# First cross-attention: a new order of the jobs in a batch, and a table that gives each job its PSUM bank

## The chip, the cores and the metric

The kernel runs on one core of a Trainium2 chip: TensorE (PE), VectorE (DVE), ScalarE (ACT), GpSimd (POOL) and SyncE (SP), each with a queue of its own that it works through in order. The metric is device time in microseconds of one execution, as the median of several runs.

## What is computed

Two decoder layers of attention, cross-attention and feed-forward, each followed by a layer norm. Only the first cross-attention is touched. Cut to what matters:

```python
q = _ln((x @ Wq + bq).reshape(b, s1, H, HD), qn_w, qn_b)          # 16 heads of 32
kv = concatenate([y_main @ Wk + bk, y_main @ Wv + bv])             # 240 context rows
k = _ln(kv[..., :HD], kn_w, kn_b);  v = kv[..., HD:]
k_dca, v_dca = ...                                                # the same from the last 16 rows, own weights
ctx = softmax(q k^T * SCALE) v + softmax(q k_dca^T * SCALE) v_dca
x = _layernorm(x + ctx @ Wo + bo)
```

There are 8 batches of 256 rows, width 512. Both softmaxes run over the same 256 columns of scores: 240 and 16.

## The kernel before

`cross_attention_0` first prepares weights, then runs the 8 batches as a software pipeline. The work of a batch is cut into named jobs. A list (`order`) of jobs, each with a shift that says for how many batches ahead or behind it works, is one slot; `grouped_slots` makes 8 slots of it, and leaves out what would lie outside batches 0 to 7. `Plan` numbers the events. Every engine walks the same list and does its own part of each job, so the list sets the order on all five engines at once. The engines meet only through semaphores, whose counts `Plan` works out from the list.

The jobs, with u = 0 to 7 for four heads and one half of the rows, t or kt for a half of rows or keys:

- xt, yt: x or context is transposed on TensorE into a PSUM bank; ScalarE copies it, rounded, as the high half (L133), VectorE writes the rest as the low half (L139). All large products are three passes over such halves (L519).
- q(t), k(t), v(t): projections, 13 or 7 matmuls of 512 columns. For q and k ScalarE writes the squares and a copy (L919, L920), and VectorE makes the variance (L948, L950).
- qn, kn: GpSimd raises the variance to the power -0.5 and multiplies (L804, L806).
- qt, kt: four transposes; ScalarE writes a high half and a full copy (L895, L900). ql, kl: GpSimd subtracts them (L811).
- score(u): 12 matmuls into four banks kept for scores, of which there is one set, so score(u + 1) waits until exp(u) is over (L862). max(u): VectorE, the negated maximum (L954 to L960). exp(u): ScalarE, four exponentials with sums and one for the last 16 columns (L925, L928). rec(u): VectorE, the reciprocal sums (L965, L967). scale(u): GpSimd multiplies by them (L817).
- pt(u, kt): four transposes of the scaled result (L869), then high half and low half as above; av(m), m = 0 to 3: 24 matmuls of 256 columns; its result again as two halves.
- out(t): 13 matmuls; VectorE adds to x and takes statistics (L973, L163, L165), GpSimd takes the root, fin(t) applies it (L180).
- load: SyncE fetches the context of a later batch.

Four PSUM banks form a ring for all jobs but score. A job's matmuls wait until the bank's last user is read out: after the low half on VectorE, or for qt and kt after ScalarE. Which bank a job has comes from `turn`, which before is made by `bank_turns`: the ring jobs of a slot in their order take banks 0, 1, 2, 3, 0, ..., and the last three 0, 1, 2. Two temporary tiles (`temps`) are shared by q, k, qt, kt. Two tiles hold the exponentials, used by u in turn.

Of the kernel before, what the change touches and what calls it, by code (L numbers as in the profile page):

```python
# [522 lines left out]
def cross_attention_0(nc, g, ctx, a):  # L523
# [10 lines left out]
    def unit(u):
        return [(("score", u), 0), (("max", u), 0), (("exp", u), 0)]

    def turned(u, shift=0):
        return [(("pt", u, kt), shift) for kt in range(QT)]

    def ready(u):  # L540
        return [(("rec", u), 0), (("scale", u), 0)]

    order = [
        [(("ql", 0), 0), (("qt", 1), 0), *turned(7, -1), *unit(0), (("q", 0), 1), (("ql", 1), 0), *ready(0)],
        [*unit(1), (("qn", 0), 1), (("av", 3), -1), *ready(1), *turned(0), (("kt", 1), 0), (("v", 0), 0), (("kl", 1), 0)],
        [*unit(2), (("v", 1), 0), *ready(2), *turned(1), (("out", 0), -1)],
        [*unit(3), (("out", 1), -1), (("fin", 0), -1), (("av", 0), 0), *ready(3), *turned(2), (("yt",), 1), (("load",), 2)],
        [*unit(4), (("k", 0), 1), (("fin", 1), -1), *ready(4), *turned(3), (("k", 1), 1)],
        [*unit(5), (("kn", 0), 1), (("av", 1), 0), *ready(5), *turned(4)],
        [*unit(6), (("kn", 1), 1), (("q", 1), 1), *ready(6), *turned(5)],  # L550
        [(("score", 7), 0), (("kt", 0), 1), (("max", 7), 0), (("exp", 7), 0), (("qn", 1), 1), (("av", 2), 0), (("kl", 0), 1),
         *ready(7), *turned(6), (("xt", 0), 2), (("xt", 1), 2), (("qt", 0), 1)]]
# [1884 lines left out]
```

## Time and profile before

| what | value |
|---|---|
| median of 3 runs | 2538.05 us (2537.85 to 2539.27) |
| the profiled execution | 2538.91 us |
| its span, first to last instruction | 2537.0 us |
| mean granted TensorE clock | 0.933 |
| TensorE, VectorE, ScalarE, GpSimd busy | 2159.8, 1568.4, 1215.2, 762.9 us |
| the batches of the first cross-attention | about 505 to 1012 us of the span |

Starts are counted from the span's first instruction. A matmul's end in the trace is modelled and overlaps the next one's start, so spacing of starts, not the sum of durations, tells how long a run of matmuls took. An idle time is put down to the semaphore that came last.

### The profile page before, as it was taken

The page shows a single profiled execution, that of the slowest core. Times are in us where ns is not written, and L with a number is a line of the kernel's source. Part 1 is how long each engine was busy: PE and PEld are TensorE (multiplying, and loading weights), DVE is VectorE, ACT ScalarE, POOL GpSimd, SP SyncE. Part 2 cuts the span into 40 slices and gives each one's busy share as a digit, 9 for nine tenths or more (in the row PEclk, how much of TensorE's full clock was granted, in tenths as well). Part 3 has the DMA queues.
Part 4 walks back from the last instruction along what each step waited for, and adds up shares of the span by engine and source line. Part 5 has one row for each costly group of instructions (what it writes and reads, how often), then busy time and mean ns, then how long its engine had stood idle before and what let it go on. Part 6 is the DMA issues. An engine that isn't in the chain of part 4 may idle for free. (4 is left out here: it accounts for less than half of the span.)

```text
span 2537.0 us, 40781 instructions
## 1 busy us (share of the span) xinstructions
PE 2159.8 (85%) x15664; PEld 1831.0 (72%) x15664; DVE 1568.4 (62%) x3131; ACT 1215.2 (48%) x3223; POOL 762.9 (30%) x820
## 2 busy tenths in 40 slices
PE   5999998388888887499997879999999999966876
PEld 5898897266777766377776778888988988853443
DVE  3555664555656554788875645556666666656777
ACT  3555553366666653444333334445555554423466
POOL 2233332666666652044441111111111112220011
PEclk8999999689999987599998989999999999988999
DMA  3000000200000000711101031224324312101000
GB/s 133 1 2 1 2 1 1 75 5 5 5 5 6 5 1 4 256 65 34 34 18 46 1 133 59 93 84 145 113 84 146 112 68 76 51 1 67 6 29 34
DMA packets 42777, 127.17 MB, mean 50 GB/s; under 512 B 3917, under 2 KB 11086, under 8 KB 37593
## 3 DMA queue, kind: packets, MB, share of 16 engines
q1 hardware_dynamic: 42584, 124.56, 14.0%
q8 instruction: 126, 2.06, 0.4%
q14 instruction: 67, 0.54, 0.1%
HBM read 103.57 MB, written 20.97 MB: 49 GB/s over the span
## 5 line engine op out<-in xcount | busy, mean ns | idle before, releaser
L2003 POOL TENSOR_TENSOR x_probs<-x_probs,x_total 128x512 f32<-128x512 f32 x128 | 133.2, 1041 | 595.5 <-DVE x_total L1973 595.3
L1928 ACT ACTIVATE x_probs<-banks,x_nmax 128x256 f32<-128x256 f32 x256 | 119.0, 469 | 213.9 <-DVE x_nmax L1962 213.9
L133 ACT ACTIVATE x_probsT_hi<-banks 128x512 fp32r<-128x512 f32 x256 | 143.7, 607 | 106.8 <-PE banks L1862 101.2
L519 PE MATMUL banks<-x_probsT_hi,x_V_hi 128*128 128x256 f32 x512 | 160.6, 314 | 38.6 <-DVE x_probsT_lo L139 38.0
L139 DVE TENSOR_TENSOR x_probsT_lo<-banks,x_probsT_hi 128x512 fp32r<-128x512 f32 x256 | 165.1, 675 | 45.8 <-ACT x_probsT_hi L133 45.6
L519 PE MATMUL banks<-x_turned,x_wq_hi 128*128 128x256 f32 x1024 | 186.0, 283 | 8.2 <-DVE x_turned L139 8.2
L925 ACT ACTIVATE x_probs<-banks,x_nmax 128x240 f32<-128x240 f32 x256 | 114.4, 460 | 139.8 <-DVE x_nmax L955 139.8
L817 POOL TENSOR_TENSOR x_probs<-x_probs,x_total 128x960 f32<-128x960 f32 (+1 forms) x128 | 130.4, 1040 | 161.3 <-DVE x_total L967 161.3
L448 ACT ACTIVATE a_probs<-banks,a_nmax 128x128 f32<-128x128 f32 (+1 forms) x256 | 104.1, 419 | 126.9 <-DVE a_nmax L464 126.9
L519 PEld LDWEIGHTS banks<-x_turned,x_wq_hi 128*128 128x128 f32 x1024 | 156.8, 189 | 9.4 <-DVE x_turned L139 9.4
L504 POOL TENSOR_TENSOR a_probs<-a_probs,a_total 128x512 f32<-128x512 f32 x64 | 93.9, 1467 | 229.5 <-DVE a_total L474 229.5
L519 PE MATMUL banks<-x_probsT_lo,x_V_hi 128*128 128x256 f32 x512 | 154.7, 302 | 0.0
L519 PE MATMUL banks<-x_probsT_hi,x_V_lo 128*128 128x256 f32 x512 | 154.5, 302 | 0.0
L519 PEld LDWEIGHTS banks<-x_probsT_hi,x_V_hi 128*128 128x128 f32 x512 | 107.4, 210 | 51.0 <-DVE x_probsT_lo L139 49.7
L519 PE MATMUL banks<-x_turned,x_wq_lo 128*128 128x256 f32 x512 | 143.6, 280 | 0.0
L1279 POOL TENSOR_TENSOR f_hid_lo<-f_hid,f_hid_hi 128x256 fp32r<-128x256 f32 x128 | 93.8, 734 | 138.6 <-ACT f_hid_hi L133 138.6
L1260 ACT ACTIVATE f_act<-f_z 128x256 f32<-128x256 f32 x128 | 53.4, 417 | 149.8 <-DVE f_z L1331 149.8
L1242 PE MATMUL banks<-f_downT,f_hid_hi 128*128 128x512 f32 x256 | 111.0, 434 | 0.0
L519 PEld LDWEIGHTS banks<-x_probsT_hi,x_V_lo 128*128 128x128 f32 x512 | 108.2, 211 | 0.0
L519 PEld LDWEIGHTS banks<-x_probsT_lo,x_V_hi 128*128 128x128 f32 x512 | 107.9, 211 | 0.3
L519 PE MATMUL banks<-x_wo_hi,x_oT_hi 128*128 128x512 f32 x256 | 105.0, 410 | 2.1 <-DVE x_oT_lo L139 2.1
L140 DVE SCALAR_TENSOR_TENSOR x_qT_lo<-banks,x_qT_hi 128x512 fp32r<-128x512 f32 x64 | 44.3, 692 | 99.4 <-ACT x_qT_hi L133 99.4
(455 smaller groups left out, 7245.6 us busy)
## 6 DMA issues: line engine op xcount, KB each, us to landing
x_turned<-x_parked SPq DMA_DIRECT2D x24, 1536.0 KB, 6.8
x_parked<-x_turned SPq DMA_DIRECT2D x8, 1536.0 KB, 5.8
x_raw_q<-in_L_xattn_Wq_dram SPq DMA_DIRECT2D x5, 1024.0 KB, 5.2
x_raw_o<-in_L_xattn_Wo_dram SPq DMA_DIRECT2D x5, 1024.0 KB, 8.2
x_all<-in_x_dram SPq DMA_DIRECT2D x2, 2048.0 KB, 18.7
x_ys<-in_ctx_dram SPq DMA_DIRECT2D x16, 256.0 KB, 2.9
f_raw<-in_L_ffn_W_g_dram SPq DMA_DIRECT2D x4, 1024.0 KB, 7.0
f_raw<-in_L_ffn_W_u_dram SPq DMA_DIRECT2D x4, 1024.0 KB, 5.4
```

Source lines behind the costliest of these rows:

```text
L133: return eng.activation(out, in_, ACT.Copy, scale=scale)
L139: return eng.tensor_tensor(out, in_, high.bitcast(F32), ALU.subtract)
L448: ins = eng.activation(probs[u % NP][:, r, 0:keys], banks[:, r, :], ACT.Exp, bias=nmax[:, u, r:r + 1], accum_out=total[:, u, r:r + 1])
L504: eng.tensor_tensor(probs[u % NP][:, :, 0:keys], probs[u % NP][:, :, 0:keys], total[:, u, :].unsqueeze(2).to_broadcast([P, G4, keys]), ALU ...
L519: ins = eng.matmul(out, lhs, rhs, start=start and n == 0, stop=stop and n == len(steps) - 1)
L817: ins = eng.tensor_tensor(tile, tile, total[:, u, n, :].unsqueeze(2).to_broadcast([P, G4, c1 - c0]), ALU.mult)
L925: eng.activation(probs[u % NP][:, r, 0:MAIN], g.S[:, r, 0:MAIN], ACT.Exp, bias=nmax[:, u, r:r + 1], accum_out=total[:, u, 0, r:r + 1])
L1242: ins = eng.matmul(g.S[:, 2 * b.parity + t, :], h[:, t * P:(t + 1) * P], downT[:, m, :], start=m == 0 and n == 0, stop=m == HT - 1 and n == 1)
L1260: eng.activation(act[zb][:, :], z[zb][:, :], ACT.Silu).then_inc(silued, 1)
L1279: eng.tensor_tensor(hid_lo[buf][:, :], hid[buf][:, :], hid_hi[buf][:, :].bitcast(F32), ALU.subtract).then_inc(low, 1)
L1928: ins = eng.activation(probs[t][r][:, j, :], g.S[:, 2 * t + r, j * S:(j + 1) * S], ACT.Exp, bias=nmax[:, t, r, j:j + 1], accum_out=total[: ...
L2003: eng.tensor_tensor(probs[t][r][:, :, :], probs[t][r][:, :, :], total[:, t, r, :].unsqueeze(2).to_broadcast([P, 2, S]), ALU.mult).then_inc ...
```

## The change

The eight sub-lists with their helpers `unit`, `turned` and `ready` go; one flat list of the same 86 jobs with the same shifts takes their place. And `turn` comes from a table of four lists, one for each bank, instead of `bank_turns`. No job, instruction or tile is added or removed. Lines below the edit move down by nine (L817 becomes L826, L869 becomes L878).

```diff
-    order = [
-        [(("ql", 0), 0), (("qt", 1), 0), *turned(7, -1), *unit(0), (("q", 0), 1), (("ql", 1), 0), *ready(0)],
...
-    steps = [((s, *job), shift) for s, jobs in enumerate(order) for job, shift in jobs]
+        (("pt", 7, 0), -1), (("pt", 7, 1), -1), (("qt", 1), 0), (("ql", 0), 0), (("score", 0), 0), (("ql", 1), 0),
...
+        (("kl", 0), 1), (("fin", 1), -1)]
+    steps = [((0, *job), shift) for job, shift in order]
...
-    turn = bank_turns([(job[0], *job[2:]) for job in slots[1] if job[0] in ring])
+    banks = [
+        [
+            ("qt", 1), ("v", 0), ("out", 0), ("pt", 2, 1), ("pt", 3, 1), ("pt", 4, 0), ("q", 1), ("pt", 6, 0),
+            ("xt", 0)],
+        [
+            ("pt", 7, 1), ("av", 3), ("pt", 0, 0), ("v", 1), ("out", 1), ("yt",), ("k", 1), ("pt", 5, 1), ("av", 2),
+            ("xt", 1)],
+        [
+            ("pt", 0, 1), ("pt", 1, 0), ("av", 0), ("k", 0), ("pt", 3, 0), ("av", 1), ("pt", 5, 0), ("kt", 0),
+            ("qt", 0)],
+        [
+            ("pt", 7, 0), ("q", 0), ("kt", 1), ("pt", 1, 1), ("pt", 2, 0), ("pt", 4, 1), ("pt", 6, 1)]]
+    turn = {job: n for n, jobs in enumerate(banks) for job in jobs}
```

TensorE's jobs in a slot read, before: qt1, pt7, score0, q0, score1, av3, pt0, kt1, v0, score2, v1, pt1, out0, score3, out1, av0, pt2, yt, score4, k0, pt3, k1, score5, av1, pt4, score6, q1, pt5, score7, kt0, av2, pt6, xt0, xt1, qt0 (in a slot before, ql(0) stands ahead of qt(1)). After: pt7, qt1, score0, q0, av3, score1, pt0, kt1, v0, score2, v1, pt(1, 0), out0, pt(1, 1), score3, out1, av0, yt, pt2, score4, k0, pt3, score5, k1, av1, pt4, score6, pt5, q1, score7, kt0, av2, pt(6, 0), xt1, pt(6, 1), qt0, xt0.

Three places, as the built programs have them, all in a batch in the middle of the stage. First TensorE from the last matmul of k(0) on. `x0_probs1` is the tile of pt(3, .), `kT` and `qT` belong to score(5), `wk` to k(1). Before:

```order
L519 MATMUL banks<-x0_bias,x0_select_k0 128x512
L869 MATMUL banks<-ident,x0_probs1 128x128 [waits x0_probs_scaled,x0_bank_done]
L869 MATMUL banks<-ident,x0_probs1 128x128 x3
L869 MATMUL banks<-ident,x0_probs1 128x128 [waits x0_probs_scaled,x0_bank_done]
L869 MATMUL banks<-ident,x0_probs1 128x128 x3
L519 MATMUL banks<-x0_wk_hi,x0_yT_hi 128x512 [waits x0_bank_done]
```

and after:

```order
L519 MATMUL banks<-x0_bias,x0_select_k0 128x512
L878 MATMUL banks<-ident,x0_probs1 128x128 [waits x0_probs_scaled,x0_bank_done]
L878 MATMUL banks<-ident,x0_probs1 128x128 x3
L878 MATMUL banks<-ident,x0_probs1 128x128 [waits x0_probs_scaled,x0_bank_done]
L878 MATMUL banks<-ident,x0_probs1 128x128 x3
L871 MATMUL banks<-x0_kT_hi,x0_qT_hi 128x256 [waits x0_probs_ready,x0_low_split]
L871 MATMUL banks<-x0_kT_hi,x0_qT_hi 128x256 x3
L871 MATMUL banks<-x0_kT_lo,x0_qT_hi 128x256 x4
L871 MATMUL banks<-x0_kT_hi,x0_qT_lo 128x256 x4
L519 MATMUL banks<-x0_wk_hi,x0_yT_hi 128x512 [waits x0_bank_done]
```

score(5) has moved ahead of k(1); that pt(3, 0) now has the bank of k(0) shows only in the table of banks.

Second, GpSimd at the end of a slot. `x0_probs0` is the tile of scale(6) and `x0_probs1` that of scale(7); `hst_q1` and `normal_q1` are qn(1); `kT_lo` is kl(0), the two `qT_lo` are ql(0) and ql(1). Before:

```order
L817 TENSOR_TENSOR x0_probs0<-x0_probs0,x0_total 128x4x240 [waits x0_rtotals_ready]
L817 TENSOR_TENSOR x0_probs0<-x0_probs0,x0_total 128x4x16
L804 TENSOR_TENSOR x0_hst_q1<-x0_hst_q1,minus_half 128x16 [waits x0_variance_ready]
L806 TENSOR_TENSOR x0_normal_q1<-x0_normal_q1,x0_hst_q1 128x512 [waits x0_qk_roots]
L811 TENSOR_TENSOR x0_kT_lo<-x0_temp0,x0_kT_hi 128x512 [waits x0_high_split]
L817 TENSOR_TENSOR x0_probs1<-x0_probs1,x0_total 128x4x240 [waits x0_rtotals_ready]
L817 TENSOR_TENSOR x0_probs1<-x0_probs1,x0_total 128x4x16
L811 TENSOR_TENSOR x0_qT_lo<-x0_temp1,x0_qT_hi 128x512 [waits x0_high_split]
L811 TENSOR_TENSOR x0_qT_lo<-x0_temp0,x0_qT_hi 128x512 [waits x0_high_split]
```

and after:

```order
L826 TENSOR_TENSOR x0_probs0<-x0_probs0,x0_total 128x4x240 [waits x0_rtotals_ready]
L826 TENSOR_TENSOR x0_probs0<-x0_probs0,x0_total 128x4x16
L813 TENSOR_TENSOR x0_hst_q1<-x0_hst_q1,minus_half 128x16 [waits x0_variance_ready]
L815 TENSOR_TENSOR x0_normal_q1<-x0_normal_q1,x0_hst_q1 128x512 [waits x0_qk_roots]
L826 TENSOR_TENSOR x0_probs1<-x0_probs1,x0_total 128x4x240 [waits x0_rtotals_ready]
L826 TENSOR_TENSOR x0_probs1<-x0_probs1,x0_total 128x4x16
L820 TENSOR_TENSOR x0_kT_lo<-x0_temp0,x0_kT_hi 128x512 [waits x0_high_split]
L820 TENSOR_TENSOR x0_qT_lo<-x0_temp1,x0_qT_hi 128x512 [waits x0_high_split]
L820 TENSOR_TENSOR x0_qT_lo<-x0_temp0,x0_qT_hi 128x512 [waits x0_high_split]
```

kl(0) has moved from ahead of scale(7) to behind it.

Third, VectorE at the start of a slot. `nmax` is the maximum of max(0), `total` is rec(0), `hst_q0` the statistics of q(0), `attT_lo` the low half of av(3); the second `dscore` copy begins max(1). Before:

```order
L955 TENSOR_REDUCE x0_nmax<-banks 128x4
L958 TENSOR_REDUCE x0_dmax<-x0_dscore 128x4 [waits x0_link]
L960 TENSOR_TENSOR x0_dscore<-x0_dscore,x0_dmax 128x64 [waits x0_link]
L948 TENSOR_REDUCE x0_hst_q0<-x0_temp1 128x16 [waits x0_squares_ready]
L950 TENSOR_SCALAR x0_hst_q0<-x0_hst_q0 128x16 [waits x0_bank_done]
L965 TENSOR_REDUCE x0_total<-x0_probs0 128x4 [waits x0_probs_ready]
L967 RECIPROCAL x0_total<-x0_total 128x8 [waits x0_link]
L954 COPY x0_dscore<-banks 128x64 [waits x0_scores_ready]
L955 TENSOR_REDUCE x0_nmax<-banks 128x4
```

and after:

```order
L964 TENSOR_REDUCE x0_nmax<-banks 128x4
L967 TENSOR_REDUCE x0_dmax<-x0_dscore 128x4 [waits x0_link]
L969 TENSOR_TENSOR x0_dscore<-x0_dscore,x0_dmax 128x64 [waits x0_link]
L974 TENSOR_REDUCE x0_total<-x0_probs0 128x4 [waits x0_probs_ready]
L976 RECIPROCAL x0_total<-x0_total 128x8 [waits x0_link]
L957 TENSOR_REDUCE x0_hst_q0<-x0_temp1 128x16 [waits x0_squares_ready]
L959 TENSOR_SCALAR x0_hst_q0<-x0_hst_q0 128x16 [waits x0_bank_done]
L139 TENSOR_TENSOR x0_attT_lo<-banks,x0_attT_hi 128x256 [waits x0_high_split]
L963 COPY x0_dscore<-banks 128x64 [waits x0_scores_ready]
L964 TENSOR_REDUCE x0_nmax<-banks 128x4
```

rec(0) has moved ahead of the statistics of q(0), and av(3) ahead of max(1). rec(6) and q(1) have changed places in the same way.

## Rows read from the trace of the kernel before

**Rows 1.** Timeline, TensorE: start, duration, line, operation, count, idle before and releaser.
```profile
605.07 0.39 PE L519 MATMUL banks<-x_probsT_hi,x_V_hi 128*128 128x256 f32 x1 [0.77 <-DVE x_probsT_lo L139]
...
608.03 1.04 PE L869 MATMUL banks<-ident,x_probs 128*128 128x128 f32 x8
...
609.77 0.50 PE L519 MATMUL banks<-x_wq_hi,x_xT_hi 128*128 128x512 f32 x1
...
612.90 1.03 PE L869 MATMUL banks<-ident,x_probs 128*128 128x128 f32 x8
...
619.20 0.42 PE L519 MATMUL banks<-x_probsT_lo,x_V_hi 128*128 128x256 f32 x1
...
626.30 1.12 PE L869 MATMUL banks<-ident,x_probs 128*128 128x128 f32 x8
628.11 0.39 PE L862 MATMUL banks<-x_kT_hi,x_qT_hi 32*128 32x256 f32 x4 [0.69 <-POOL x_qT_lo L811]
...
660.42 1.03 PE L869 MATMUL banks<-ident,x_probs 128*128 128x128 f32 x8
```

**Rows 2.** Timeline, GpSimd, the whole stage.
```profile
516.12 2.04 POOL L817 TENSOR_TENSOR x_probs<-x_probs,x_total 128x960 f32<-128x960 f32 x2 [7.51 <-DVE x_total L967]
...
574.70 2.04 POOL L817 TENSOR_TENSOR x_probs<-x_probs,x_total 128x960 f32<-128x960 f32 x2 [6.03 <-DVE x_total L967]
...
616.90 2.04 POOL L817 TENSOR_TENSOR x_probs<-x_probs,x_total 128x960 f32<-128x960 f32 x2 [0.64 <-DVE x_total L967]
618.90 2.89 POOL L804 TENSOR_TENSOR x_hst_q<-x_hst_q,minus_half 128x16 f32<-128x16 f32 x1
...
622.88 1.28 POOL L811 TENSOR_TENSOR x_kT_lo<-x_temp,x_kT_hi 128x512 fp32r<-128x512 f32 x1
624.12 2.04 POOL L817 TENSOR_TENSOR x_probs<-x_probs,x_total 128x960 f32<-128x960 f32 x2
...
635.44 2.04 POOL L817 TENSOR_TENSOR x_probs<-x_probs,x_total 128x960 f32<-128x960 f32 x2 [6.03 <-DVE x_total L967]
...
991.31 2.04 POOL L817 TENSOR_TENSOR x_probs<-x_probs,x_total 128x960 f32<-128x960 f32 x2 [6.07 <-DVE x_total L967]
```

**Rows 3.** Table of stretches: us, then each engine's busy time, TensorE's granted clock.
```profile
core 0: us, PE busy (x) PEld busy (x) DVE busy (x) ACT busy (x) POOL busy (x), PEclk, DMA share, GB/s
603.50:664.24 60.74, 52.11 (x378) 43.33 (x376) 37.35 (x91) 38.55 (x118) 38.69 (x32) 0.97 0.02 5
724.98:785.72 60.74, 52.10 (x373) 43.77 (x374) 36.54 (x87) 38.19 (x118) 38.74 (x32) 0.94 0.02 5
907.20:967.94 60.74, 48.60 (x341) 41.27 (x340) 34.27 (x85) 34.74 (x107) 34.90 (x30) 0.86 0.00 1
622.50:628.70 6.20, 4.75 (x47) 3.79 (x45) 3.23 (x8) 5.88 (x11) 5.49 (x6) 1.00 0.00 0
```

**Rows 4.** TensorE's waits from 603.5 to 664.24: total us, times, longest.
```profile
PE banks L862 <- ACT x_probs L928: 2.1, 2, 1.3
```

**Rows 5.** Timeline, VectorE, one period.
```profile
610.08 1.24 DVE L139 TENSOR_TENSOR x_probsT_lo<-banks,x_probsT_hi 128x512 fp32r<-128x512 f32 x2
...
611.36 1.15 DVE L955 TENSOR_REDUCE x_nmax<-banks 128x4 f32<-128x960 f32 x1
...
615.57 0.69 DVE L948 TENSOR_REDUCE x_hst_q<-x_temp 128x16 f32<-128x512 f32 x1 [2.68 <-ACT x_normal_q L920]
...
616.37 0.21 DVE L965 TENSOR_REDUCE x_total<-x_probs 128x4 f32<-128x64 f32 x1
```

**Rows 6.** Timeline, ScalarE, the same period.
```profile
608.95 0.39 ACT L133 ACTIVATE x_attT_hi<-banks 128x256 fp32r<-128x256 f32 x1
609.21 1.10 ACT L133 ACTIVATE x_probsT_hi<-banks 128x512 fp32r<-128x512 f32 x2
612.54 0.46 ACT L925 ACTIVATE x_probs<-banks,x_nmax 128x240 f32<-128x240 f32 x1 [2.23 <-DVE x_nmax L955]
```

**Rows 7.** DMA issues of the page: count, KB each, us from issue to landing.
```profile
x_ys<-in_ctx_dram SPq DMA_DIRECT2D x16, 256.0 KB, 2.9
```

More of the change, by code:

```diff
@@ L532, in cross_attention_0 @@
     NP = 2
[L534 to L541, printed above, removed]
-    order = [
-        [(("ql", 0), 0), (("qt", 1), 0), *turned(7, -1), *unit(0), (("q", 0), 1), (("ql", 1), 0), *ready(0)],
[L545 to L552, printed above, removed]
@@ L553, in cross_attention_0 @@
-    steps = [((s, *job), shift) for s, jobs in enumerate(order) for job, shift in jobs]
+    order = [
+        (("pt", 7, 0), -1), (("pt", 7, 1), -1), (("qt", 1), 0), (("ql", 0), 0), (("score", 0), 0), (("ql", 1), 0),
+        (("max", 0), 0), (("exp", 0), 0), (("rec", 0), 0), (("q", 0), 1), (("av", 3), -1), (("score", 1), 0),
+        (("max", 1), 0), (("scale", 0), 0), (("exp", 1), 0), (("rec", 1), 0), (("pt", 0, 0), 0), (("pt", 0, 1), 0),
+        (("qn", 0), 1), (("kt", 1), 0), (("v", 0), 0), (("score", 2), 0), (("max", 2), 0), (("scale", 1), 0),
+        (("v", 1), 0), (("pt", 1, 0), 0), (("out", 0), -1), (("exp", 2), 0), (("rec", 2), 0), (("pt", 1, 1), 0),
+        (("score", 3), 0), (("max", 3), 0), (("scale", 2), 0), (("out", 1), -1), (("fin", 0), -1), (("exp", 3), 0),
+        (("av", 0), 0), (("kl", 1), 0), (("yt",), 1), (("rec", 3), 0), (("scale", 3), 0), (("pt", 2, 0), 0),
+        (("pt", 2, 1), 0), (("score", 4), 0), (("max", 4), 0), (("k", 0), 1), (("kn", 0), 1), (("exp", 4), 0),
+        (("rec", 4), 0), (("pt", 3, 0), 0), (("pt", 3, 1), 0), (("score", 5), 0), (("max", 5), 0), (("exp", 5), 0),
+        (("rec", 5), 0), (("scale", 4), 0), (("k", 1), 1), (("av", 1), 0), (("pt", 4, 0), 0), (("pt", 4, 1), 0),
+        (("scale", 5), 0), (("score", 6), 0), (("max", 6), 0), (("kn", 1), 1), (("pt", 5, 0), 0), (("pt", 5, 1), 0),
+        (("load",), 2), (("exp", 6), 0), (("rec", 6), 0), (("q", 1), 1), (("score", 7), 0), (("kt", 0), 1),
+        (("max", 7), 0), (("exp", 7), 0), (("av", 2), 0), (("rec", 7), 0), (("scale", 6), 0), (("pt", 6, 0), 0),
+        (("xt", 1), 2), (("qn", 1), 1), (("scale", 7), 0), (("pt", 6, 1), 0), (("qt", 0), 1), (("xt", 0), 2),
+        (("kl", 0), 1), (("fin", 1), -1)]
```

## Prediction

> **What bounds the kernel now.** I write times inside a batch as "at x", counted from the moment at which TensorE starts the two transposes pt(7, .), the first ring jobs of the new list. In the trace that moment is 626.30, and one period earlier 565.56 [rows 1].
>
> First the table by stretches. The stage runs in periods of 60.74 us: the same multiplication of u = 0 starts on GpSimd at 574.70 and at 635.44 [rows 2]. In one period TensorE is busy 52.1 us, the other three engines 37 to 39 us [rows 3]. So TensorE has the most work, but 8.6 us of a period it stands idle, and its waits are spread over several releasers, the largest 2.1 us in sum [rows 4]. No single wait is the bound; what closes the period is a ring of hand-overs.
>
> Second, the clock. TensorE's granted clock averages 0.97 in one period and 0.94 in another, and both last 60.74 us [rows 3]. At 0.94 the clock spent about 7.3 us at its lower level (0.06 x 2 x 60.74), at 0.97 about 3.6 us; a matmul of 256 columns in that stretch has 0.42 us (619.20 [rows 1]). The extra slow time changed the period by nothing. Something that is not TensorE closes it.
>
> Third, GpSimd's timeline at the end of a period. It is busy without a gap from 616.90: scale(6), then the power and product of qn(1), then kl(0) at 622.88, then scale(7) at 624.12, which ends at 626.16, and pt(7, 0) follows at 626.30 [rows 1, 2]. scale(6) was released by rec(6) on VectorE at 616.37 [rows 5]. exp(6) had ended at 614.56, 2.02 us after it began at 612.54 [rows 6]; rec(6) then lay behind VectorE's statistics of q(1), which wait for ScalarE to write q(1) and start only at 615.57 [rows 5, 6]. So the period ends: max(6), exp(6), q(1) on ScalarE and VectorE, rec(6), scale(6), qn(1), kl(0), scale(7).
>
> **The change part by part.** No instruction is added or removed: the terms are moves.
>
> Part a, score(5) goes ahead of k(1). Before, k(1) with its 13 matmuls stands between pt(3, .) and score(5); 13 such matmuls take 3.13 us (609.77 to 612.90 [rows 1]). Before, exp(5) occupies ScalarE until 608.95, and so the copies of av(1) and of pt(4, .) start only then and at 609.21 [rows 6], though av(1) had started at 605.07 and its 24 matmuls took 2.96 us, to 608.03 [rows 1]. With exp(5) over early, the copy starts as soon as av(1) and the transpose are through, and max(6), last at 611.36 [rows 5], can be asked for 1.0 us earlier: at 44.7 for its copy instead of 45.7. This needs av(1) to start no later than now, at 39.5. I walked the new list by hand from 0, each job in its engine's order, with the durations of the rows: 3.13 us for 13 matmuls and 2.9 for av [rows 1], 2.02 for an exp and 0.55 for a copy on ScalarE [rows 6], 1.15 for a maximum, 0.62 for a low half and 0.8 for the statistics of q or k on VectorE [rows 5], 2.04 for a multiplication on GpSimd, 3.98 for qn or kn and 1.24 for kl or ql [rows 2]. Stations: score(0) at 2.5, av(3) 6.3, pt(0, 0) 10.2, score(2) 13.6, out(0) 18.3, av(0) 25.6, pt(3, 0) 34.4, score(5) 35.5, k(1) 36.2, av(1) 39.4. That is level with before. **Gain 1.0 us.**
>
> Part b, rec(6) goes ahead of q(1), and pt(5, .) ahead of exp(6). rec(6) no longer waits for q(1)'s statistics: 616.37 against the end of exp(6) at 614.56 [rows 5, 6], **gain 1.8 us**. q(1) itself, its 3.13 us of matmuls now after pt(5, .), is copied right behind exp(6) on ScalarE (from 47.9), its statistics are done by 49.9, and max(7) by then is next. What is late then is qn(1): it holds GpSimd 2.89 us for the power and 1.05 for the product (618.90 to 622.88 [rows 2]), from 50.6 to 54.6; rec(7) is ready at 54.3. So scale(7) starts at 54.6.
>
> Part c, kl(0) goes behind scale(7). It takes 1.24 us of GpSimd (622.88 to 624.12 [rows 2]) out of the chain before pt(7, 0): **gain 1.2 us**. It comes back behind: kl(0) and ql(0) now both stand between scale(7) and score(0), so score(0) starts 2.5 after pt(7, 0) and not 1.81 (628.11 less 626.30 [rows 1]). The walk absorbs these 0.7 us, because av(3) now stands ahead of score(1) and fills what before was a wait for exp(0), part of the 2.1 us of the first row of waits [rows 4].
>
> The rest moves for nothing. load goes from slot position 4 of 8 to behind pt(5, .), some 40 us before the next yt; one fetch lands in 2.9 us [rows 7], so its margin is large, and without it yt would wait those 2.9. fin(1) goes to the end, half a microsecond of VectorE behind xt(0)'s low half, which is what qt(1) waits for; kn(0), kn(1), kl(1) and scale(4) change places on GpSimd in a stretch in which nobody waits for them.
>
> Together 4.0 us: scale(7) ends at 56.7 where it ended at 60.6, a period of 56.8 us with the clock at its upper level.
>
> Part d, the banks. The old turn gives each ring job the bank used three or four ring jobs earlier. The table puts k(0) and pt(3, 0) in the same bank, one straight behind the other. Before, pt(3, 0) follows k(0) without idle, at 660.42 [rows 1]. Now it waits until VectorE has read k(0)'s squares, which lie behind max(4): 2.2 us of idle. I cost it at nothing, because score(5) right behind waits until 35.5 for exp(4), while pt(3, 1) is over at 35.3. The cover is 0.2 us thin; without it the price is up to 2.2 us a period. The Trainium skill, "Perfetto Trace Analysis", section "Optimizing Tensor Performance", speaks against this part: independent matmul groups should rotate through different PSUM banks, so that emptying one overlaps the next group. By that rule the full 2.2 us would be lost; in my walk they lie in time that TensorE would wait anyway. No row of the kernel before shows such a pair.
>
> Part e, the clock. Before, low-clock time was free. In the new list matmuls of q(0), av(3), k(1) and av(1) are on the path, so it is not free everywhere. If the new list has as much low-clock time as the old (3.6 to 7.3 us a period), it loses 1.8 to 3.6 us of TensorE's time, of which a part falls under waits (the bank wait, and from 52 to 59, where TensorE has little but transposes). The bounds are 0 and 3.6; I take 1.2, a third of the larger, as before's slow time stood beside waits. Period: 58.0 us, 2.7 less.
>
> **The sum.** Six whole periods (574.70 to 939.14): 16.4 us. The first batch took 58.58 us (516.12 to 574.70 [rows 2]) and has no pt(7, .), av(3) or out: 2 us. The last batch runs from scale(7) at 927.8 (624.12 plus five periods) to scale(7) at 991.31 [rows 2], 63.5 us though q, k, xt and yt are gone, at a clock of 0.86 in most of it [rows 3]. It is a pure chain of hand-overs, with av at half clock; rec(u) no longer behind other work should give 3 to 7 us, and I take 4. Total 22.4. The profiled execution, 2537.0 us of span and 1.9 around it, becomes 2514.6 and 1.9; the median of the runs lies 0.9 below that execution: **2515.5 us**.
>
> **Rivals.** *The clock stays up on the path.* Then the period is 56.8 and the sum 6 x 3.9 + 3 + 4 = 30.6, **2507.5 us**. For it: the idle time is less in total. Against: the new list gathers it at two places.
>
> *The banks cost what they show.* If pt(3, 0) is released later than max(4) suggests, or pt(0, 0) and v(1), which also stand behind the job that they need emptied, the 2.2 us come through: 22.4 less 6 x 2.2 leaves 9.2, **2529 us**. For it: a cover of only 0.2 us. Against: it needs VectorE late there, and VectorE is busy only 37 of 60.7 us [rows 3].
>
> *The clock takes it all back.* All 3.6 us on the path make a period of 60.4; with 3 us from the ends the gain is 5 or less, **2534 us**, no change.
>
> *The clock falls at the turn of the batch: slower.* From 52 to 59 TensorE has transposes, three waits and one score. If the low clock that follows lies on q(0) and av(3) entirely, their 6.0 us take 12.0, and nothing hides that, since score(1) now stands behind av(3) where before it stood ahead. Period 62.8, six times 2.1 more, no gain at the ends: **2550.5 us**. It decides from 4 us of loss a period, 8 us of matmuls at the lower level on the path. Against: before, the zone of transposes from 622.5 to 628.7 ran at a granted clock of 1.00 [rows 3].
>
> **How the numbers follow.** Forecast 0.50 (its own range 2508 to 2524), clock up 0.17, banks or another wait I walked past 0.17, clock takes all 0.10, slower 0.06. The range of 2502 to 2533 leaves out the last two and the end of the second. A measurement of this kernel can tell about 0.2% (5.1 us) from no change: faster by more 0.82, within 0.11, slower by more 0.07.
>
> **What would show it.** In the trace after: equal distances of about 58 between the multiplications of one u on GpSimd (57 with the clock up, over 60 if I am wrong); kl(0) straight behind scale(7); rec(6) straight behind exp(6); an idle entry of TensorE of about 2 us at the transposes of pt(3, 0), released by VectorE's reduction of k(0); score(5) starting within 0.3 us of pt(3, 1). I am wrong if the period is not 2 to 4 us shorter, if the 2 us at pt(3, 0) push k(1) back, or if q(0) and av(3) run at 0.42 us a matmul in most batches.

## The result and the profile after

The changed kernel takes 2506.98 us (median of four runs, 2502.97 to 2511.61). The kernel before, run on the same chip, takes 2538.66 us (2537.85 to 2539.67). The ratio is 0.9876, with a 95% interval of 0.9858 to 0.9893: about 31.7 us, or 1.2%, faster. The forecast was 2515.5 us with a range of 2502 to 2533. The profiled execution of the changed kernel took 2502.97 us, the fastest of its four. Below, "before" and "after" are the two profiled executions, and "scale(0)" is the first GpSimd multiplication of a batch.

The page of the profile after begins so (busy us, share of the span, instructions):

```profile
PE 2135.3 (85%) x15657; PEld 1810.9 (72%) x15664; DVE 1596.3 (64%) x3131; ACT 1218.3 (49%) x3223; POOL 763.3 (31%) x820
```

GpSimd's timeline after. The lines of before that answer to it are [rows 2]; every line number is nine higher.

```profile
510.73 2.04 POOL L826 TENSOR_TENSOR x_probs<-x_probs,x_total 128x960 f32<-128x960 f32 x2 [3.68 <-DVE x_total L976]
...
564.54 2.04 POOL L826 TENSOR_TENSOR x_probs<-x_probs,x_total 128x960 f32<-128x960 f32 x2 [1.68 <-DVE x_total L976]
...
624.82 2.04 POOL L826 TENSOR_TENSOR x_probs<-x_probs,x_total 128x960 f32<-128x960 f32 x2 [2.24 <-DVE x_total L976]
...
667.82 2.89 POOL L813 TENSOR_TENSOR x_hst_q<-x_hst_q,minus_half 128x16 f32<-128x16 f32 x1
670.79 1.05 POOL L815 TENSOR_TENSOR x_normal_q<-x_normal_q,x_hst_q 128x512 f32<-128x512 f32 x1
672.06 2.04 POOL L826 TENSOR_TENSOR x_probs<-x_probs,x_total 128x960 f32<-128x960 f32 x2 [0.22 <-DVE x_total L976]
674.06 1.27 POOL L820 TENSOR_TENSOR x_kT_lo<-x_temp,x_kT_hi 128x512 fp32r<-128x512 f32 x1
...
681.86 2.04 POOL L826 TENSOR_TENSOR x_probs<-x_probs,x_total 128x960 f32<-128x960 f32 x2 [2.23 <-DVE x_total L976]
...
960.26 2.22 POOL L826 TENSOR_TENSOR x_probs<-x_probs,x_total 128x960 f32<-128x960 f32 x2 [4.03 <-DVE x_total L976]
```

At the end of a batch GpSimd now does qn(1), scale(7) and only then kl(0). From the starts of scale(0), 510.73, 564.54, ..., 913.86 after and 516.12, 574.70, ..., 940.57 before, comes the account of the gain:

| stretch | before, us | after, us | gain | forecast |
|---|---|---|---|---|
| start of the program to the first scale(0) | 516.12 | 510.73 | 5.4 | 0 |
| first batch | 58.58 | 53.81 | 4.8 | 2 |
| six whole periods | 365.87 | 349.32 | 16.55 | 16.4 |
| last scale(0) to last scale(7) | 50.74 | 46.40 | 4.3 | 4 |
| behind the stage, to the end | 1545.7 | 1540.8 | 4.9 | 0 |

The last row is the span less the last scale(7), 2537.0 less 991.31 and 2501.1 less 960.26. No instruction there has changed, and in the profiled executions of the twelve kernels below, which have the same instructions there, this part takes 1544.2 (e9) to 1547.5 us (e2), and no less in e1 (1547.2), which differs from the changed kernel by one entry of the table. So the 4.9 us can't be put down to the change, and what makes this part shorter or longer stays open. The first four rows add up to 31.05 us, close to the 31.7 between the medians.

The six periods by stretch of time, first after, then before (all but its fourth and fifth, 61.61 and 61.54 us, both at 0.94). Columns: us, each engine's busy time, then TensorE's granted clock, DMA share and GB/s.

```profile
564.54:624.82 60.28, 53.38 (x381) 44.38 (x380) 41.02 (x90) 39.12 (x119) 38.74 (x32) 0.94 0.02 5
624.82:681.86 57.04, 50.12 (x378) 41.86 (x378) 41.38 (x90) 39.01 (x119) 38.70 (x33) 1.00 0.02 6
681.86:740.18 58.32, 51.60 (x379) 43.07 (x378) 41.20 (x90) 39.11 (x119) 38.70 (x32) 0.97 0.02 5
740.18:797.23 57.05, 50.12 (x379) 41.88 (x378) 41.38 (x90) 39.01 (x119) 38.70 (x32) 1.00 0.02 6
797.23:855.53 58.30, 51.58 (x379) 42.90 (x378) 41.33 (x90) 39.11 (x119) 38.70 (x33) 0.97 0.02 6
855.53:913.86 58.33, 51.15 (x383) 43.02 (x381) 40.63 (x89) 38.17 (x116) 38.86 (x33) 0.94 0.00 1
```

```profile
574.70:635.44 60.74, 52.11 (x378) 43.33 (x377) 37.36 (x92) 38.55 (x118) 38.70 (x32) 0.97 0.02 5
635.44:695.92 60.48, 52.07 (x378) 43.07 (x377) 37.44 (x92) 38.74 (x118) 38.59 (x32) 0.97 0.02 5
695.92:757.70 61.78, 53.16 (x378) 44.41 (x377) 37.48 (x92) 38.56 (x118) 38.72 (x32) 0.94 0.02 5
...
880.85:940.57 59.72, 47.47 (x340) 39.51 (x342) 35.33 (x86) 36.49 (x114) 38.72 (x32) 0.91 0.00 1
```

Two things stand here. A period after lasts 57.04 us with the clock at its upper level throughout (1.00), and 58.32 at 0.97: one low stretch costs 1.3 us. And before, too, the low clock had a price: 60.6 at 0.97, but 61.5 to 61.8 at 0.94. The first five periods gain 15.16 us, 3.0 each; the sixth, which leads into the last batch, gains 1.39. With the same mean clock in both, a period is 2.3 us shorter at 0.97 (60.6 less 58.3) and 1.4 at 0.94 (61.6 less 60.28). The rest of the mean of 2.76 (16.55 / 6) goes with the clock: none of the six periods before is without a low stretch, two of those after are.

TensorE after, at the points that the prediction named:

```profile
617.29 1.09 PE L878 MATMUL banks<-ident,x_probs 128*128 128x128 f32 x8 [0.70 <-DVE x_probsT_lo L139]
...
651.62 1.09 PE L878 MATMUL banks<-ident,x_probs 128*128 128x128 f32 x8 [1.90 <-DVE x_hst_k L957]
652.90 0.39 PE L871 MATMUL banks<-x_kT_hi,x_qT_hi 32*128 32x256 f32 x4 [0.19 <-ACT x_probs L937]
...
674.34 1.09 PE L878 MATMUL banks<-ident,x_probs 128*128 128x128 f32 x8 [0.70 <-DVE x_probsT_lo L139]
```

With pt(7, .) at 617.29 as zero, pt(3, .) starts at 34.3 (the walk had 34.4), behind 1.90 us of idle released by VectorE's statistics of k(0), and score(5) at 35.6 (the walk had 35.5). In the rows of GpSimd above, qn(1) starts at 50.5 (the walk had 50.6) and scale(7) at 54.8 (54.6). The wait totals of TensorE from 510 to 985 after (us, times, longest):

```profile
PE banks L878 <- DVE x_hst_k L957: 13.3, 7, 1.9
PE banks L871 <- ACT x_probs L937: 12.4, 22, 3.3
PE banks L841 <- DVE x_attT_lo L139: 10.6, 6, 1.8
PE banks L878 <- POOL x_probs L826: 8.7, 5, 2.8
```

and the four largest of before over the same stretch:

```profile
PE banks L862 <- ACT x_probs L928: 19.7, 20, 4.5
PE banks L519 <- DVE x_probsT_lo L139: 15.0, 17, 2.0
PE banks L869 <- POOL x_probs L817: 14.1, 11, 4.1
PE banks L519 <- DVE x_ydT_lo L139: 8.7, 7, 1.2
```

The new first row of after, 13.3 us, is the bank that pt(3, 0) shares with k(0); the third, 10.6, is xt(1), which the table puts in the bank of av(2). The row that is gone without my having given it a price is the fourth of before: k(0) waiting for the low half of yt.

### The profile page after: what moved, and what is told of

Same layout as the page of the kernel before. It is cut to its first block and busy times, and to the rows that moved or that the text cites. A ratio compares the mean times of both kernels' runs of the same rounds, so it can differ in the third digit from the quotient of the medians.

```text
span 2501.1 us, 40774 instructions
## 1 busy us (share of the span) xinstructions
PE 2135.3 (85%) x15657; PEld 1810.9 (72%) x15664; DVE 1596.3 (64%) x3131; ACT 1218.3 (49%) x3223; POOL 763.3 (31%) x820
## 5 line engine op out<-in xcount | busy, mean ns | idle before, releaser
L519 PE MATMUL banks<-x_probsT_hi,x_V_hi 128*128 128x256 f32 x512 | 151.4, 296 | 25.0 <-DVE x_probsT_lo L139 24.4
L826 POOL TENSOR_TENSOR x_probs<-x_probs,x_total 128x960 f32<-128x960 f32 (+1 forms) x128 | 130.9, 1043 | 74.1 <-DVE x_total L976 74.1
L519 PE MATMUL banks<-x_probsT_hi,x_V_lo 128*128 128x256 f32 x512 | 147.1, 287 | 0.0
L519 PE MATMUL banks<-x_probsT_lo,x_V_hi 128*128 128x256 f32 x512 | 147.0, 287 | 0.0
L519 PEld LDWEIGHTS banks<-x_probsT_hi,x_V_hi 128*128 128x128 f32 x512 | 100.0, 195 | 33.3 <-DVE x_probsT_lo L139 32.0
L519 PE MATMUL banks<-x_wo_hi,x_oT_lo 128*128 128x512 f32 x256 | 101.1, 395 | 0.0
L519 PE MATMUL banks<-x_wo_lo,x_oT_hi 128*128 128x512 f32 x256 | 101.0, 395 | 0.0
```

The lines of the kernel that those rows point to most:

```text
L519: ins = eng.matmul(out, lhs, rhs, start=start and n == 0, stop=stop and n == len(steps) - 1)
L826: ins = eng.tensor_tensor(tile, tile, total[:, u, n, :].unsqueeze(2).to_broadcast([P, G4, c1 - c0]), ALU.mult)
```

## The experiments

Twelve kernels, each beside the kernel before on its chip (medians 2537.15, 2537.56 and 2538.32 us in the three groups). "1.00" and "0.97" are a period (scale(0) to scale(0)) at that granted clock; "last" is the start of the last scale(7).

| kernel | median us | ratio [95%] | 1.00 | 0.97 | first scale(0) | six periods | last |
|---|---|---|---|---|---|---|---|
| before | 2538.66 | 1 | | 60.6 | 516.12 | 365.87 | 991.31 |
| after | 2506.98 | .9876 [.9858, .9893] | 57.04 | 58.3 | 510.73 | 349.32 | 960.26 |
| e1 | 2506.99 | .9879 [.9863, .9896] | 57.03 | 58.5 to 58.8 | 511.47 | 347.96 | 957.95 |
| e2 | 2508.41 | .9887 [.9872, .9901] | 56.97 | 58.5 | 511.59 | 347.71 | 957.70 |
| e3 | 2582.02 | 1.0175 [1.016, 1.019] | | 66.96 | 514.89 | 407.64 | 1035.32 |
| e4 | 2544.08 | 1.0025 [1.0014, 1.0036] | | 61.95 | 514.44 | 374.23 | 1000.43 |
| e5 | 2523.98 | .9941 [.9923, .9958] | | 59.6, 60.5 | 510.19 | 362.33 | 977.95 |
| e6 | 2524.06 | .9945 [.993, .996] | 58.97 | 60.5 | 515.35 | 356.87 | 978.90 |
| e7 | 2522.48 | .9939 [.9922, .9956] | 59.52 | 59.8, 60.5 | 516.38 | 356.57 | 979.05 |
| e8 | 2530.09 | .9972 [.9963, .9982] | 59.19 | 60.80 | 513.34 | 363.68 | 980.85 |
| e9 | 2509.61 | .9887 [.9873, .9902] | 56.81 | 58.08 | 512.41 | 350.30 | 961.75 |
| e10 | 2511.81 | .9898 [.9883, .9912] | 57.52 | 58.92 | 516.30 | 346.54 | 965.83 |
| e11 | 2515.80 | .9912 [.9896, .9929] | 58.8 | 58.82 | 512.13 | 353.71 | 965.68 |
| e12 | 2510.66 | .9887 [.9872, .9902] | 58.25 | 58.30 | 511.42 | 349.48 | 962.20 |

Up to the first scale(0) many of these kernels have the same list, and its start still varies by some 2 us: 510.73 after, 511.42 to 512.41 in e1, e2, e9, e11 and e12. So differences of that size in this column can't be put down to the list.

**The bank wait, e1.** The changed kernel, with pt(3, 0) taken out of k(0)'s bank:

```diff
-            ("pt", 0, 1), ("pt", 1, 0), ("av", 0), ("k", 0), ("pt", 3, 0), ("av", 1), ("pt", 5, 0), ("kt", 0),
+            ("pt", 0, 1), ("pt", 1, 0), ("av", 0), ("k", 0), ("av", 1), ("pt", 5, 0), ("kt", 0),
...
-            ("pt", 7, 0), ("q", 0), ("kt", 1), ("pt", 1, 1), ("pt", 2, 0), ("pt", 4, 1), ("pt", 6, 1)]]
+            ("pt", 7, 0), ("q", 0), ("kt", 1), ("pt", 1, 1), ("pt", 2, 0), ("pt", 3, 0), ("pt", 4, 1), ("pt", 6, 1)]]
```

> The changed kernel, with pt(3, 0) moved in the table from the bank of k(0) to the bank that pt(2, 0) used. My theory: the 1.9 us of idle behind k(0) are free while the clock is up (score(5) would wait for exp(4) anyway), so the distance of the multiplications of scale(0) stays at 57.0 us in periods at full clock; but if that idle is what brings the clock down in some periods (58.3 us, clock 0.97), those fall to 57.0 too, and the time falls by 3 to 6 us against the changed kernel. Rival (the bank wait costs what it shows): the full-clock period falls by 1 to 2 us, to 55 to 56, and the time by 7 to 12 us.

2506.99 us, no difference. TensorE's timeline in e1, a batch at full clock; its scale(0) is at 624.15:

```profile
649.71 1.06 PE L878 MATMUL banks<-ident,x_probs 128*128 128x128 f32 x8 [0.67 <-POOL x_probs L826]
652.22 0.39 PE L871 MATMUL banks<-x_kT_hi,x_qT_hi 32*128 32x256 f32 x4 [1.44 <-ACT x_probs L937]
```

pt(3, .) starts 25.56 us after scale(0) instead of 26.80, and score(5) starts 28.07 after it, as in the changed kernel (28.08). The wait has moved one job on. The bank wait is fully covered, as costed. The periods of e1 at 0.97 did not fall to 57.0, so the idle time behind k(0) is not what brings the clock down.

**The table alone, e2 and e3.** e2 is the new order with the old turn, e3 the old order with the new table:

```diff
-    turn = {job: n for n, jobs in enumerate(banks) for job in jobs}
+    turn = bank_turns([(job[0], *job[2:]) for job in slots[1] if job[0] in ring])
```

> The new order with banks by the old turn. My theory: the gain is the order's; full-clock period 57.0 within 0.3 us, time within 5 us of the changed kernel's 2507. Rival (the table of banks is worth something of its own): period 58 us or more, 2513 us or more.

> The old order with the new table of banks. My theory: nothing gained; pt(3, 0) right behind k(0) in one bank now waits until exp(4) and k(0)'s statistics are through, about 3.2 us later than now, ahead of k(1) and score(5): period 62 to 64 us, time 2546 to 2560 us. Rival (the table gives the gain): below 2530 us.

e2: 2508.41 us. The table brings nothing that can be told from zero; the whole gain is the order's. TensorE's waits in e2 have neither the row of k(0)'s bank nor that of xt(1), 23.9 us together in the changed kernel. Instead two other rows are twice what they were there; the waits have gone to other jobs:

```profile
PE banks L871 <- ACT x_probs L937: 24.5, 25, 3.3
PE banks L878 <- POOL x_probs L826: 19.4, 18, 2.8
```

e3: 2582.02 us, 44.9 slower than before, far more than the 2546 to 2560 that I expected. TensorE's waits in e3 from 510 to 1000:

```profile
PE banks L881 <- DVE x_hst_k L960: 21.4, 7, 3.1
PE banks L881 <- DVE x_attT_lo L139: 15.5, 7, 2.4
PE banks L863 <- DVE x_probsT_lo L139: 14.4, 8, 2.0
```

Not one pair collides but at least three: pt(3, 0) behind k(0), pt(0, 0) behind av(3), and a kt or qt behind a pt. The table fits one order. The same 2-to-3 us wait behind k(0) that is free in the new order is not covered in the old one, where k(1) stands straight behind pt(3, .), and not a score that waits anyway.

**The three moves, e4.** Before, with only a (score(5) ahead of k(1)), b (pt(5, .) ahead of exp(6), rec(6) ahead of q(1)) and c (kl(0) behind scale(7)), which the prediction gave 4.0 us a period:

```diff
-        [*unit(4), (("k", 0), 1), (("fin", 1), -1), *ready(4), *turned(3), (("k", 1), 1)],
-        [*unit(5), (("kn", 0), 1), (("av", 1), 0), *ready(5), *turned(4)],
-        [*unit(6), (("kn", 1), 1), (("q", 1), 1), *ready(6), *turned(5)],
-        [(("score", 7), 0), (("kt", 0), 1), (("max", 7), 0), (("exp", 7), 0), (("qn", 1), 1), (("av", 2), 0), (("kl", 0), 1),
-         *ready(7), *turned(6), (("xt", 0), 2), (("xt", 1), 2), (("qt", 0), 1)]]
+        [*unit(4), (("k", 0), 1), (("fin", 1), -1), *ready(4), *turned(3)],
+        [*unit(5), (("k", 1), 1), (("kn", 0), 1), (("av", 1), 0), *ready(5), *turned(4)],
+        [(("score", 6), 0), (("max", 6), 0), (("kn", 1), 1), *turned(5), (("exp", 6), 0), (("rec", 6), 0), (("q", 1), 1), (("scale", 6), 0)],
+        [(("score", 7), 0), (("kt", 0), 1), (("max", 7), 0), (("exp", 7), 0), (("qn", 1), 1), (("av", 2), 0),
+         *ready(7), (("kl", 0), 1), *turned(6), (("xt", 0), 2), (("xt", 1), 2), (("qt", 0), 1)]]
```

> The kernel before with only three moves: score(5) ahead of k(1), pt(5, .) ahead of exp(6) and rec(6) ahead of q(1), kl(0) behind scale(7). My theory: these are the three terms; period 57 to 58 us and 2513 to 2520 us, the rest of the gain being in the first and last batch. Rival (the gain comes from the front half of the list: av(3) ahead of score(1), rec(0) ahead of q(0)): period above 59.5 us, 2530 us or more.

2544.08 us: slower than before by 0.25%, the interval clear of 1. GpSimd and TensorE in e4:

```profile
667.74 2.91 POOL L804 TENSOR_TENSOR x_hst_k<-x_hst_k,minus_half 128x16 f32<-128x16 f32 x1
670.72 1.05 POOL L806 TENSOR_TENSOR x_normal_k<-x_normal_k,x_hst_k 128x512 f32<-128x512 f32 x1
672.73 2.04 POOL L817 TENSOR_TENSOR x_probs<-x_probs,x_total 128x960 f32<-128x960 f32 x2 [0.96 <-DVE x_total L967]
...
674.91 1.94 PE L869 MATMUL banks<-ident,x_probs 128*128 128x128 f32 x8 [3.49 <-POOL x_probs L817]
```

The last row is pt(5, .), moved ahead of q(1). It needs scale(5), which stands behind kn(0) on GpSimd and waits for rec(5), which VectorE does behind its work for k(1) and av(1). Before, q(1)'s matmuls filled that time; now TensorE stands for 3.49 us (3.2 to 3.5 in seven of the eight batches), and q(1) is late as well.

**kn(0) and rec(5) added, e7.** e4, plus kn(0) right behind k(0), and rec(5), scale(5) ahead of k(1) and av(1):

```diff
-        [*unit(4), (("k", 0), 1), (("fin", 1), -1), *ready(4), *turned(3)],
-        [*unit(5), (("k", 1), 1), (("kn", 0), 1), (("av", 1), 0), *ready(5), *turned(4)],
+        [*unit(4), (("k", 0), 1), (("kn", 0), 1), (("fin", 1), -1), *ready(4), *turned(3)],
+        [*unit(5), *ready(5), (("k", 1), 1), (("av", 1), 0), *turned(4)],
```

> The kernel of the three moves, with two more: kn(0) directly behind k(0), and rec(5), scale(5) directly behind exp(5), ahead of k(1) and av(1). Theory now: in the run of the three moves pt(5, .) waited 3.5 us a period for scale(5), which stood behind kn(0) and, on VectorE, behind k(1) and av(1); with both out of its way the wait goes and the moves pay: period 57.5 to 59.5 us, 2515 to 2525 us. Rival (something else in the old order holds the three moves back): period still 61 us or more, no faster than 2535 us.

2522.48 us, 21.6 below e4. The two moves turn a loss into half of the gain. kn(0) is among the jobs that the prediction said "change places on GpSimd in a stretch in which nobody waits for them"; that rec(5) and scale(5) move ahead of k(1) and av(1) it doesn't mention at all. Which of the two carries how much was not tried.

**Halves of the list, e5 and e6.** e5 has the new list up to pt(2, 1) and the old behind it; e6 the old list up to yt and the new from score(4) on; both the old turn. The lists are too long to show; they are those of the two kernels cut at score(4).

> The list of the changed kernel up to pt(2, 1), then the old list from score(4) on; banks by the old turn. Theory now: the old end of a batch (k(1), q(1), rec(6), kl(0)) sets the turn, so whole periods stay at 60 to 61 us; but the first batch gains what the changed kernel gains there (first scale at 511 to 512 instead of 516, since rec(0) no longer waits for q(0)'s statistics). Time 2525 to 2535 us. Rival (the first half carries the gain): periods 57 to 58.5 us, 2515 us or less.

> The old list up to its slot 3, then the new list from score(4) on; banks by the old turn. Theory now: moves a to c work only together with kn(0), rec(5) and scale(5) at their new, earlier places, all in this half; whole periods 57.5 to 59.5 us, the first scale of the stage still at 514 to 516; time 2515 to 2525 us. Rival: above 60 us a period, 2532 us or more.

Each half brings about 13.5 us (2523.98, 2524.06), and both together 28.7 (e2, against 2537.15). So the first half, which the prediction called "level with before", is worth as much as the second in the whole time, but not in the same place. Of e5's gain 5.9 us lie ahead of the first scale(0) and 3.5 in the six periods; of e6's, 0.8 and 9.0. e2 has 18.2 in the six periods, more than both together: in whole periods the second half carries more, and each half gains by the other. e5 came out 1 us below the total expected of it, e6 within its own; e6's periods at 0.97 (60.5) are a microsecond longer than was expected.

**The start of a batch, e8 and e10.** The changed order, with q(0) back ahead of rec(0) and av(3) back behind exp(1); e8 with the new table, e10 with the old turn:

```diff
-        (("max", 0), 0), (("exp", 0), 0), (("rec", 0), 0), (("q", 0), 1), (("av", 3), -1), (("score", 1), 0),
-        (("max", 1), 0), (("scale", 0), 0), (("exp", 1), 0), (("rec", 1), 0), (("pt", 0, 0), 0), (("pt", 0, 1), 0),
+        (("max", 0), 0), (("exp", 0), 0), (("q", 0), 1), (("rec", 0), 0), (("score", 1), 0), (("max", 1), 0),
+        (("scale", 0), 0), (("exp", 1), 0), (("av", 3), -1), (("rec", 1), 0), (("pt", 0, 0), 0), (("pt", 0, 1), 0),
```

> The changed kernel with the start of a batch as before: q(0) ahead of rec(0), and av(3) behind score(1), max(1), exp(1). My theory: score(1) now waits for exp(0) again and the late score(0) is no longer covered, so whole periods at full clock are 58 to 59.5 us instead of 57.0; the first scale of the stage comes 2 to 4 us later. Time 2514 to 2525 us. Rival (those two moves are worth nothing in whole periods): 57.0 us at full clock, 2509 to 2512 us.

> The start of a batch undone as in the run before, but with banks by the old turn, in which pt(0, 0) doesn't share the bank of av(3). In that run (periods of 59.2 us at full clock) TensorE waited 2.4 us a period for av(3)'s low half at the transposes of pt(0, .). Theory A (the start of the order is worth about 2 us a period): still 58.5 to 59.5 us. Theory B (it was the bank that made the loss, the order of the start is worth little): 57.0 to 58.0 us.

e8: 2530.09 us, which looks as if the start were worth 23. But its TensorE waits at pt(0, 0), which in the new table has the bank of av(3), and av(3) now stands right ahead of it:

```profile
632.44 1.51 PE L878 MATMUL banks<-ident,x_probs 128*128 128x128 f32 x8 [2.43 <-DVE x_attT_lo L139]
```

With the old turn (e10) that row is

```profile
631.74 1.06 PE L866 MATMUL banks<-ident,x_probs 128*128 128x128 f32 x8 [0.69 <-POOL x_probs L814]
```

and the time 2511.81. So theory B holds, and both expectations for e8 miss its 2530. The start of the order is worth some 3 us in all, which the intervals don't tell from zero (the ratios of e10 and e2 differ by 0.0011). The traces show where it lies: 4.7 until the first scale(0) (516.30 against 511.59), 1.2 of which are there before the stage begins (first transposes of yt at 478.73 and 477.55), 2.1 in the first batch (55.73 against 53.66), and 0.55 in a period at full clock. Against it stands that one of e10's six periods is longer than at full clock, and four of e2's. Of e8's loss, 18.3 us is the bank, 1.67 us a period (59.19 less 57.52).

**The middle.** e6 and e10 differ between rec(1) and score(4), in the places of qn(0) and load, and in the order of ql, qt(1), pt(7, .) and scale(0) at the very start; e6's period at full clock is 1.45 us longer. TensorE in e6, then in e10 (scale(0) at 573.98 and 572.03):

```profile
597.23 0.50 PE L519 MATMUL banks<-x_wk_hi,x_yT_hi 128*128 128x512 f32 x1 [1.25 <-DVE x_ydT_lo L139]
```

```profile
594.14 0.50 PE L519 MATMUL banks<-x_wk_hi,x_yT_hi 128*128 128x512 f32 x1
```

Where yt stands behind pt(2, .), k(0) waits 1.25 us for its low half and starts 23.25 us after scale(0). Where yt stands ahead of pt(2, .), it starts at 22.11. kn(0) follows at 27.27 and at 26.14, scale(5) at 33.99 and at 32.86: the 1.13 us pass through GpSimd unchanged. This is read from two traces; yt was not moved by itself, so that it makes most of the 1.45 us is argued and not shown.

**kl(0), e9.** The changed kernel with move c undone, kl(0) ahead of scale(7):

```diff
-        (("xt", 1), 2), (("qn", 1), 1), (("scale", 7), 0), (("pt", 6, 1), 0), (("qt", 0), 1), (("xt", 0), 2),
-        (("kl", 0), 1), (("fin", 1), -1)]
+        (("xt", 1), 2), (("qn", 1), 1), (("kl", 0), 1), (("scale", 7), 0), (("pt", 6, 1), 0), (("qt", 0), 1), (("xt", 0), 2),
+        (("fin", 1), -1)]
```

> The changed kernel with kl(0) ahead of scale(7) again, all else kept. My theory (part c): the wrap is a chain on GpSimd, so pt(7, 0) comes 1.2 us later, of which score(0) gives 0.7 back; whole periods at full clock 57.5 to 58.3 us instead of 57.0. Time 2509 to 2516 us. Rival (kl(0)'s place is worth nothing, since ql(0) must follow it anyway before score(0)): 57.0 to 57.2 us.

2509.61 us, and a period of 56.81 at full clock, 0.23 shorter than with move c. The total can't be told from the changed kernel's (ratios 0.9887 and 0.9876). c is worth nothing: what kl(0) gives scale(7) it takes from score(0), which needs kl(0) and ql(0). In both kernels the next score(0) starts 51.9 us after scale(0) (678.15 less 626.26, and 676.70 less 624.82), though pt(7, .) starts 0.9 us later in e9 (50.40 against 49.52).

**A better list, e11 and e12.** In the new list exp(4) stands behind k(0), and score(5) waits for it. e11 (old turn) puts exp(4) ahead of k(0); e12 puts rec(4) and scale(4) there too:

```diff
-        (("pt", 2, 1), 0), (("score", 4), 0), (("max", 4), 0), (("k", 0), 1), (("kn", 0), 1), (("exp", 4), 0),
+        (("pt", 2, 1), 0), (("score", 4), 0), (("max", 4), 0), (("exp", 4), 0), (("k", 0), 1), (("kn", 0), 1),
```

> The new order with old banks and exp(4) ahead of k(0): TensorE's order is unchanged, but ScalarE does exp(4) before it copies k(0). In the run with old banks exp(4) began right behind k(0)'s copy and score(5) waited for it; it can begin about 1 us earlier. But kn(0) then comes about 2 us later and scale(4) stands behind it on GpSimd. Theory: the two cancel, 56.8 to 57.5 us at full clock. Rival: ScalarE's order alone sets it, 55.8 to 56.3 us.

> As the run before, with rec(4) and scale(4) also ahead of k(0) and kn(0), so that scale(4) doesn't wait for kn(0). Theory: score(5) about 1 us earlier and nothing taken back: 55.8 to 56.5 us at full clock, 2498 to 2504 us. Rival (scale(5), which now stands behind kn(0) alone, or the end of the batch sets the period): 57.0 us, 2506 to 2509 us.

2515.80 and 2510.66 us against e2's 2508.41 (ratios 0.9912, 0.9887 and 0.9887): neither gains, and their periods at full clock, 58.8 and 58.25, lie above theory and rival of both. Both push kn(0) back. GpSimd in e12, scale(0) at 626.25:

```profile
656.85 2.91 POOL L801 TENSOR_TENSOR x_hst_k<-x_hst_k,minus_half 128x16 f32<-128x16 f32 x1
```

kn(0) starts 30.60 after scale(0) instead of 27.03 (651.85 less 624.82 in the changed kernel), and the period is 58.25 at full clock against 56.97. A period of e12 is as long at 0.97 as at 1.00, and kn(0) starts 30.60 after scale(0) in it too (831.57 less 800.97): there the low stretch is free. No list was found that beats the changed one; e1, e2, e9 and e12 can't be told from it.

## Why the prediction was right, and where it was not

**The sign and the range** held; of the size, 31.7 us were measured between the medians where the sum had 22.4. Six periods brought 16.55 us where the sum had 16.4, and the last batch 4.3 where it had 4. But the agreement over the six is in part luck: the mean period was 60.98 before, not 60.74, and 58.22 after, not 58.0, and the two errors cancel. That the median, 2506.98, lies on the price of the rival "clock stays up" (2507.5) is luck as well: the clock didn't stay up, and what the sum lacked lies ahead of the six periods.

**The walk** of the new list was good: 56.8 us forecast, 57.04 measured at full clock, pt(3, .), score(5), qn(1) and scale(7) within 0.2 us of their stations, so what it says of the new period stands. The last batch's "63.5 us" doesn't: the scale(7) before it stood at 930.87, not at 927.8, so the stretch took 60.44 us, and 56.23 after.

**The period before was misread.** "Both last 60.74" rested on windows that I had cut myself at 60.74 us [rows 3]; the distances of scale(0) in GpSimd's timeline were 60.5 to 60.7 at a clock of 0.97 and 61.5 to 61.8 at 0.94. So "the extra slow time changed the period by nothing" was wrong; a second low stretch cost about 1.0 us before as well. Taking that off 60.6 for the first puts before at about 59.6 at full clock (an estimate; no period of before shows it). The order's gain at equal clock is then 1.4 at 0.94, 2.3 at 0.97 and by the estimate 2.6 at 1.00, not 4.0. Even that is no pure price of the order, since the low stretches lie at different jobs: before mostly in av(2) (619.20 in [rows 1]), after mostly at pt(3, .) and k(1).

**Parts a, b and c** are the steps that failed. Alone they make the kernel slower (e4), and c is worth nothing even in the new list (e9). The walk compared two ends of the same chain and handed the difference to the three moves that I could see in that chain. The moves a and b pay only with others beside them: kn(0) right behind k(0), and rec(5) and scale(5) ahead of k(1) and av(1) (e7 against e4, 21.6 us for both). And the first half of the list, priced at nothing, brings 13.6 us (e5), 5.9 of them ahead of the first scale(0), for the most part by rec(0) ahead of q(0); yt ahead of pt(2, .) is likely another part, argued from two traces. Rows for two of these were there: TensorE's waits for the low half of yt, 8.7 us in seven waits, and GpSimd's idle time of 7.51 us ahead of the first scale(0) [rows 2]. rec(6) does now stand straight behind exp(6), as the VectorE timeline after shows (compare 616.37 in [rows 5]), with q(1)'s statistics behind it:

```profile
723.60 0.22 DVE L974 TENSOR_REDUCE x_total<-x_probs 128x4 f32<-128x64 f32 x1 [0.49 <-ACT x_probs L937]
723.86 0.20 DVE L976 RECIPROCAL x_total<-x_total 128x8 f32<-128x8 f32 x1
724.58 0.69 DVE L957 TENSOR_REDUCE x_hst_q<-x_temp 128x16 f32<-128x512 f32 x1 [0.52 <-ACT x_normal_q L929]
```

The move was made as described; it pays only because scale(5) is early enough for pt(5, .).

**Part d, the banks,** held: 1.9 us of idle at pt(3, .), released by VectorE, and free (e1). The Trainium skill, "Perfetto Trace Analysis", section "Optimizing Tensor Performance", has independent groups rotate through different banks so that emptying one overlaps the next. In the new order that rule would have saved nothing (2506.99 against 2506.98 us); in e3 and e8, where what follows the wait isn't itself late, breaking it cost 44.9 and 18.3 us. The rival "the banks cost what they show" falls for this list and is right for others.

**Part e, the clock:** 1.2 us a period forecast. Measured, periods at 0.97 are 1.3 us longer than at 1.00, the first one, at 0.94, 3.2 longer, and of six periods two had no low stretch; the mean over the six, 58.22 less 57.04, is 1.2 us, as forecast, though the forecast's third was a guess. The rival "clock up" was the truth in those two. The rival "clock falls at the turn of the batch" is wrong for five of the six periods: where they have a low stretch, it begins at pt(3, .) or just behind. Only in the sixth does a second one lie at the turn (a clock of 0.83 and 0.74 from 904 to 908 and from 908 to 912, where pt(7, .) starts at 906.39), and that period, 58.33 us, is no longer than others with one. What the prediction held against this rival, a clock of 1.00 from 622.5 to 628.7, was one batch: in the next, pt(7, .), score(0) and the start of q(0), from 686 to 691, have 0.66.

**The ends.** The start (5.4 us) and 2.8 of the first batch were missing from the sum. Of the 5.4, 1.4 exist before the stage begins (the first transposes of yt at 476.89 and 478.27); in the other kernels, the same up to there, they start between 475.46 and 478.73, so this is no effect of the change. The rest is rec(0), which no longer stands behind the statistics of q(0): GpSimd waits 3.68 us for it instead of 7.51. From those transposes to the first scale(0) it is 33.8 us after (510.73 less 476.89), 37.9 before, and 37.9 again in e8 (513.34 less 475.46), which undoes this and the place of av(3); a first batch has no av(3). The first batch ran at a granted clock of 1.00 after and 0.91 before, which the sum had no term for. How much of the first batch's 4.8 us is order and how much clock was not separated. These 8.2 us and the 4.9 behind the stage, less the 0.9 that the forecast took off for the median, are 12.2 of the 12.5 us between 2515.5 and the profiled 2502.97.
